# Attention maxima: one head in a slot of one bank, four slots, in place of two heads in a slot of two banks, two slots

## The reference

```python
x = x + _L0_attn_ref(_layernorm(x), Wq_down, Wk_down, Wv_down, Wq_up_c, ..., Wv_up, Wc)
x = x + _L0_ffn_ref(_layernorm(x), Wr, br, W1, b1, W2, b2)

# in the attention, for each batch and head (q, k, v from latent projections, half of q and k with rope)
scores = einsum('bhqd,bhkd->bhqk', q, k) / sqrt(16)
scores = where(causal, scores, -inf)
att = softmax(scores, axis=-1)
y = einsum('bhqk,bhkd->bhqd', att, v)
```

## Time and profile before

| | us |
|---|---|
| three runs | 2732.42, 2733.09, 2741.71 |
| their median | 2733.09 |
| profiled execution, span from the first to the last instruction | 2735.5 |
| attention in it, about | 258 to 1941 |

### The profile page before, as it was taken

The page is one execution under the profiler, slowest core; times in us unless marked ns, Lnnn a source line. Parts: engine busy times, 40 slices in busy tenths (PEclk is TensorE's granted clock), DMA queues, the critical chain, the costliest instruction groups (busy, mean ns, idle before and its releaser), DMA issues. The chain is left out here.

```text
span 2735.5 us, 48214 instructions
## 1 busy us (share of the span) xinstructions
PE 2406.9 (88%) x15842; PEld 1359.7 (50%) x15842; DVE 2048.1 (75%) x5002; ACT 1581.1 (58%) x2716; POOL 823.7 (30%) x1130
## 2 busy tenths in 40 slices
PE   6885799999999999999999999998777389998998
PEld 6774333333334333333334333332444278887897
DVE  3876989998999898888898998940355457765776
ACT  3663277777777776667777777776433234433443
POOL 1543011211212112111212112121055655555554
PEclk8997699999999999989999999997888689999999
DMA  3777814414504513504414423010675323323332
GB/s 145 261 260 212 113 39 63 74 42 61 86 29 64 86 34 59 84 27 65 83 35 64 80 44 71 8 31 20 236 203 177 94 92 113 107 93 96 111 109 72
DMA packets 147501, 255.95 MB, mean 94 GB/s; under 512 B 72951, under 2 KB 91897, under 8 KB 138916
## 3 DMA queue, kind: packets, MB, share of 16 engines
q1 hardware_dynamic: 114544, 164.96, 27.1%
q0 software_dynamic: 29904, 80.65, 8.9%
q10 hardware_dynamic: 2812, 7.26, 1.5%
HBM read 147.59 MB, written 107.76 MB: 93 GB/s over the span
## 5 line engine op out<-in xcount | busy, mean ns | idle before, releaser
L836 ACT ACTIVATE prob<-ps_s 128x512 f32<-128x512 f32 (+5 forms) x1620 | 1078.1, 714 | 480.5 <-PE ps_s L932 477.8
L857 DVE TENSOR_REDUCE maxes<-ps_m 128x2 f32<-128x1024 f32 x768 | 913.9, 1221 | 107.8 <-PE ps_m L973 104.8
L932 PE MATMUL ps_s<-q_st,k_st 50*128 50x512 f32 (+3 forms) x2560 | 610.2, 413 | 73.8 <-ACT prob L836 57.2
L973 PE MATMUL ps_m<-k_st,q_st 48*128 48x512 f32 (+3 forms) x2560 | 603.2, 443 | 75.9 <-DVE maxes L857 39.6
L953 PE MATMUL ps_o<-prob,v_sb 128*17 128x512 f32 (+3 forms) x5120 | 617.5, 556 | 1.2 <-ACT prob L836 0.7
L802 POOL TENSOR_SCALAR_AFFINE_SELECT prob<-prob 128x256 f32<-128x256 f32 x512 | 203.2, 406 | 1347.8 <-ACT prob L836 1220.8
L973 PEld LDWEIGHTS ps_m<-k_st,q_st 48*128 48x128 f32 x2560 | 272.6, 191 | 531.3 <-DVE maxes L857 256.6
L861 DVE CUSTOM_DVE_ANT_0 junk<-ps_m,causal 128x128 f32<-128x128 f32 (+3 forms) x1024 | 453.1, 484 | 44.2 <-PE ps_m L973 42.7
L932 PEld LDWEIGHTS ps_s<-q_st,k_st 50*128 50x128 f32 x2560 | 318.3, 190 | 306.1 <-ACT prob L836 234.1
L1728 ACT ACTIVATE h_hi<-ps_turned 128x512 fp32r<-128x512 f32 x142 | 85.0, 598 | 225.6 <-PE ps_turned L1843 157.9
L94 PE MATMUL ps_out<-experts_hi,h_lo 128*128 (+1 forms) x568 | 173.0, 305 | 0.0
(11 more groups left out here) (187 smaller groups left out, 3180.6 us busy)
## 6 DMA issues: line engine op xcount, KB each, us to landing
parts_dram<-parts SPq DMA_DIRECT2D x64, 512.0 KB, 3.8
q_st<-parts_dram SPq DMA_DIRECT2D x84, 256.0 KB, 8.5
k_st<-parts_dram SPq DMA_DIRECT2D x84, 256.0 KB, 18.4
v_dram<-v_out SPq DMA_DIRECT2D x16, 544.0 KB, 5.5
xin<-in_L_attn_x SPq DMA_DIRECT2D x16, 512.0 KB, 6.0
ffn_raw<-in_L_ffn_W POOLq DMA_DIRECT2D x32, 256.0 KB, 5.2
y_dram<-y_sb SPq DMA_DIRECT2D x64, 128.0 KB, 2.0
split_hi<-ffn_hi POOLq DMA_DIRECT2D x16, 512.0 KB, 3.2
```

What stands on the lines that cost most here:

```text
L836: last_exp = nc.scalar.activation(prob[:, at:at + n, lo:TB], bank[:, 0:n, lo:TB], ACT.Exp, scale=DH ** -0.5)
L857: return nc.vector.tensor_reduce(maxes[:, 2 * pair:2 * pair + 2, qt, kc], bank[:, :, :], AX.X, ALU.max)
L932: mm = nc.tensor.matmul(ps_s[k % 2][:, i, lo:TB], k_st[half(h % 2, ROWS), w % BUFS, h // 2, kt * P:(kt + 1) * P], q_st[half(h % 2, ROWS), ...
L973: mm = nc.tensor.matmul(ps_m[slot][:, i, 0:wide], q_st[half(i, STACK), w % BUFS, pair, qt * P:(qt + 1) * P], k_st[half(i, STACK), w % BUFS ...
```

## The change

A piece of the maxima is now one head: ("max", w, qt, h, kc), with the two heads of a pair one after the other. TensorE makes one matmul for it into a slot of one bank and signals it. VectorE takes it with one tensor_reduce of 128x512 or one masked reduction, and signals it. The ring has four slots of one bank. turn_max stands four pieces into the next turn. The planner models pieces of one head, in the half of TensorE's rows that belongs to the head. The number and shape of the matmuls, of the masked reductions, of the scores and of the sums are the same; the 768 reductions of 128x1024 become 1536 of 128x512. turn_max and turn_out use one bank of a slot, as they did before.

```diff
--- before.py
+++ after.py
@@ -466,10 +466,10 @@
 HALF_ROWS = 64
 EARLY = 12
 NEG = -3.0e38
-SLOTS = 2
+SLOTS = 4
 PROBS = 6
 DEEP = 3
-AHEAD = 2
+AHEAD = 4
 BUFS = 3
 HOLD = {"max": -171, "scores": -140, "sum": 0, "turn_out": -266}
 STEP_LIST = [(w, c, kt) for w in range(NG) for c in range(CH)
@@ -502,7 +502,8 @@
     out = []
     for i, (w, late) in enumerate(turns):
         tiles = range(EARLY, QT) if late else range(EARLY)
-        pieces = [("max", w, qt, pair, kc) for qt in tiles for pair in range(2) for kc in range(qt // TILES + 1)]
+        pieces = [("max", w, qt, h, kc) for qt in tiles for pair in range(2) for kc in range(qt // TILES + 1)
+                  for h in (2 * pair, 2 * pair + 1)]
         turn = [("turn_max",) + turns[i - 1]] if i else []
         out += pieces[:AHEAD] + turn + pieces[AHEAD:] + [("chain", w, late)]
     return out + [("turn_max",) + turns[-1]]
@@ -575,9 +576,8 @@
                 rows[e[1:]] = vector + 6500
             else:
                 w = piece_width(e[2], e[4])
-                end = max(columns(0, w, ready[kind]), columns(1, w, ready[kind]))
-                vector = max(end + 42, vector - 85) + (2 * w * 1.049 + 148 if e[4] < e[2] // TILES else
-                                                       2 * (w * 1.045 + 152) - 83)
+                end = columns(e[3] % 2, w, ready[kind])
+                vector = max(end + 42, vector - 85) + (w * 1.049 + 148 if e[4] < e[2] // TILES else w * 1.045 + 152)
             taken.append(vector)
         elif kind == "scores":
             plan.append(("scores", k))
@@ -643,7 +643,7 @@
         rec = sb("rec", [P, 2, TILES, GH], F32)
         ident = sb("ident2", [P, P], F32)
         causal = sb("causal", [P, TB], F32)
-        junk = sb("junk", [P, SLOTS, 2, TB], F32)
+        junk = sb("junk", [P, SLOTS, TB], F32)
         maxes = sb("maxes", [P, GH, QT, CH], F32)
         minus = sb("minus", [P, GH * EARLY], F32)
         ones = sb("ones", [PARTS, T], F32)
@@ -653,7 +653,7 @@
         minus_rows = sb("minus_rows", [GH * EARLY, PARTS, P], F32R)
 
         ps_s = [ctx.enter_context(nc.psum_tensor(f"ps_s{i}", [P, 2 - i, 512], F32)) for i in range(2)]
-        ps_m = [ctx.enter_context(nc.psum_tensor(f"ps_m{i}", [P, 2, 512], F32)) for i in range(SLOTS)]
+        ps_m = [ctx.enter_context(nc.psum_tensor(f"ps_m{i}", [P, 512], F32)) for i in range(SLOTS)]
         ps_o = ctx.enter_context(nc.psum_tensor("ps_o", [P, 512], F32))
 
         ident_made = sem("ident_made2")
@@ -851,17 +851,13 @@
 
             def take(e, slot):
 
-                _, _, qt, pair, kc = e
+                _, _, qt, h, kc = e
                 bank = ps_m[slot]
                 if kc < qt // TILES:
-                    return nc.vector.tensor_reduce(maxes[:, 2 * pair:2 * pair + 2, qt, kc], bank[:, :, :], AX.X,
-                                                   ALU.max)
+                    return nc.vector.tensor_reduce(maxes[:, h, qt, kc:kc + 1], bank[:, :], AX.X, ALU.max)
                 w = piece_width(qt, kc)
-                for i in range(2):
-                    last = nc.vector.tensor_tensor_reduce(junk[:, slot, i, 0:w], bank[:, i, 0:w],
-                                                          causal[:, TB - w:TB], 1.0, NEG, ALU.add, ALU.max,
-                                                          maxes[:, 2 * pair + i, qt, kc:kc + 1])
-                return last
+                return nc.vector.tensor_tensor_reduce(junk[:, slot, 0:w], bank[:, 0:w], causal[:, TB - w:TB], 1.0,
+                                                      NEG, ALU.add, ALU.max, maxes[:, h, qt, kc:kc + 1])
 
             for e, ring in plan_with_ring():
                 slot = ring % SLOTS
@@ -883,14 +879,14 @@
                     if j:
 
                         dve.wait_ge(rows_in, 32 * j)
-                    nc.vector.tensor_copy(minus_rows[0:n, 0, :], bank[0:n, 0, 0:P]).then_inc(high_made, 1)
+                    nc.vector.tensor_copy(minus_rows[0:n, 0, :], bank[0:n, 0:P]).then_inc(high_made, 1)
                     dve.wait_ge(high_made, j + 1)
-                    nc.vector.tensor_tensor(out=minus_rows[0:n, 1, :], in0=bank[0:n, 0, 0:P],
+                    nc.vector.tensor_tensor(out=minus_rows[0:n, 1, :], in0=bank[0:n, 0:P],
                                             in1=minus_rows[0:n, 0, :].bitcast(F32),
                                             op=ALU.subtract).then_inc(piece_taken, 1)
                 elif e[0] == "turn_out":
                     c, made = e[1] % 2, e[1] // 2
-                    src = ps_m[slot][:, 0, :].rearrange("p (j h d) -> p j h d", j=TILES, h=GH)
+                    src = ps_m[slot][:, :].rearrange("p (j h d) -> p j h d", j=TILES, h=GH)
                     dve.wait_ge(piece_made, ring + 1)
                     nc.vector.reciprocal(rec[:, c, :, :], src[:, :, :, DH]).then_inc(rec_made, 1)
                     dve.wait_ge(rec_made, e[1] + 1)
@@ -960,7 +956,7 @@
                     if ring >= SLOTS:
                         pe.wait_ge(piece_taken, ring - SLOTS + 1)
                     if e[0] == "max":
-                        _, w, qt, pair, kc = e
+                        _, w, qt, h, kc = e
                         if w == 0 and chunks_seen <= qt // TILES < 2:
                             pe.wait_ge(chunk_loaded[chunks_seen], (LOADS - 1) * 16)
                             chunks_seen += 1
@@ -969,19 +965,18 @@
                             pe.wait_ge(loaded[w % BUFS], LOADS * 16 * (w // BUFS + 1))
                             loads_seen = w + 1
                         wide = piece_width(qt, kc)
-                        for i in range(2):
-                            mm = nc.tensor.matmul(ps_m[slot][:, i, 0:wide],
-                                                  q_st[half(i, STACK), w % BUFS, pair, qt * P:(qt + 1) * P],
-                                                  k_st[half(i, STACK), w % BUFS, pair, kc * TB:kc * TB + wide],
-                                                  start=True, stop=True)
+                        mm = nc.tensor.matmul(ps_m[slot][:, 0:wide],
+                                              q_st[half(h % 2, STACK), w % BUFS, h // 2, qt * P:(qt + 1) * P],
+                                              k_st[half(h % 2, STACK), w % BUFS, h // 2, kc * TB:kc * TB + wide],
+                                              start=True, stop=True)
                     elif e[0] == "turn_max":
                         n = GH * (QT - EARLY if e[2] else EARLY)
                         pe.wait_ge(minus_made, turn_number(e[1], e[2]) + 1)
-                        mm = nc.tensor.transpose(ps_m[slot][0:n, 0, 0:P], minus[:, 0:n], ident[:, :])
+                        mm = nc.tensor.transpose(ps_m[slot][0:n, 0:P], minus[:, 0:n], ident[:, :])
                     else:
                         pe.wait_ge(out_copied, e[1] + 1)
                         for j in range(TILES):
-                            mm = nc.tensor.transpose(ps_m[slot][:, 0, j * P:(j + 1) * P],
+                            mm = nc.tensor.transpose(ps_m[slot][:, j * P:(j + 1) * P],
                                                      out_sb[:, e[1] % CH, j * P:(j + 1) * P], ident[:, :])
                     mm.then_inc(piece_made, 1)
 
```

## The result

Before 2732.76 us (median of 4 runs), after 2843.49 (2821.78 to 2860.64, 4 runs): a ratio of 1.0398, interval 1.0322 to 1.0473. I had said 2707, with a range of 2655 to 2768. The profiled execution has a span of 2858.9 us, 123 more than before.

The account below looks back on a forecast made before the run. The chain of scores, exponentials and sums was taken to bound the kernel. 2735.5 - 28 (slots) + 1.5 (VectorE) = 2709 us, as a median 2707; own range 2690 to 2722, over all cases 2655 to 2768.

Parts of the forecast that it names:

- the part on TensorE: TensorE's matmuls: number and sizes unchanged, parted pairs 0, newly computed planner order 0 with 10 us either way.
- What bounds the kernel: Attention: the chain of scores, exponentials and sums sets the end; maxima matter where they hold up TensorE's queue.
- the 51 us: VectorE: two reductions of 512 add 0.066 us per full pair, 51 us of work, only 1.5 us on the path.
- The slots: PSUM slots for maxima: banks freed one reduction earlier remove three quarters of TensorE's 37.2 us idle time, 28 us.
- Rival 2: TensorE: sums or scores between a pair's heads cost 0.10 us each, 43 us for a third of pairs; chance 0.14.

Follow-up runs that it names:

- -100: Changed kernel with the planner's allowance for maxima (HOLD) at -100 instead of -171, run twice: 0.9847 and 0.9876 of the kernel before.
- the pair order: Changed kernel's single-head slots with the old planner's list, each pair written as its two heads in a row: 0.9945, repeated on another chip 0.9991.
- -150: Changed kernel with the planner's allowance for maxima (HOLD) at -150 instead of -171: 1.0122 of the kernel before.
- the full dose: Single-head slots, old list, even heads of two successive pieces put before the odd ones, 1764 same-half neighbours instead of 682: 1.0308 of the kernel before.
- the postponed sums: Kernel before, from step 40 each sum with step number a multiple of 8 put back until just before the next sum: 1.037.
- -171: The changed kernel as it stands, with the planner's allowance for maxima (HOLD) at -171: 1.0398 of the kernel before.
- two doses: Single-head slots, old list, heads regrouped by half in every couple of pieces (1.0308) or only in every second couple (1.0126).

## Why the prediction was wrong

- *The step that failed* is the last of the part on TensorE: "The planner's order is computed anew with the same holds, and may shift some groups; I count this at 0 with 10 us either way." It was worth more than 110 us. With the old list the same slots cost nothing (0.9945 and 0.9991), with the new one 4.0%. I had treated HOLD as a constant of the kernel. It is a credit for each piece, and the change halved the piece; with -100 in its place the changed kernel is at 0.985 to 0.988.
- *What bounds the kernel* was right: the chain of steps sets the end, and VectorE's reductions don't. The two reductions cost +0.4% at the most likely, and the 51 us were 962.7 - 913.9 = 49.
- *The slots* were over-priced. TensorE's idle time for VectorE fell as forecast, from 37.2 us to 3.4 in the pair order (its rows above and 0.4 before the output transpose), but from 320 to 1815 us the busy time of the maxima matmuls rose by 57 us (566.3 to 622.8) and that of TensorE as a whole by 29, and the time fell by 0.1 to 0.55%, not 1%. That the two heads' banks now come free 0.60 us apart, so that the second matmul starts later behind the first, would explain it; this is argued, not tested.
- *Rival 2* (parted pairs) named a real cost, but as 43 us in the worst case and at 0.10 us each, where 0.065 to 0.09 in all and 0.05 at the full clock were measured. The changed kernel has 432 more same-half neighbours: 22 us at the 0.05, about half of the 47 us in slower steps. Even that half is not shown. At -150, with 1077 neighbours, a step takes 2.48 us at the full clock, as before the change, and at -100, with 978, only 2.41.
- *The clock* stood in no rival, though the two windows of before (0.98 in the middle part, 0.79 in the tail) showed that it is not constant in this kernel. Two thirds of the loss or more stand there.
- *Open*: how much of the clock's part is due to long stretches and how much to same-half neighbours (the full dose and the postponed sums had one without the other, and both had more falls), and what makes -171 so much worse than -150, where the profiled execution has 14 falls and 122 us at the lower level in its middle part. That the order of the list costs the time is shown; which feature of it costs how much is not.

The page "TensorE: Matmul & The Clock Gate" of the Trainium skill describes (section "A second HAM failure mode: psum-queue depth-cycling") a clock that swings because TensorE idles for a moment between groups of matmuls. The trace agrees in part only: before the fall shown above the idle rows are 0.17 and 0.20 us, and the middle part as a whole is busier than before the change (1546.08 of 1585 us). What was missing ahead of most of its falls was sums, not busy time; that this is the cause was not isolated.

## What to carry to other kernels

When a list is written by a planner, changing the size of a piece changes the planner: re-set the allowances before judging the change, and count in the new list what went with the loss here: stretches without full-array work, neighbours in one half of the array, and a lead at the buffers' limit. To price the hardware side alone, run the new mechanism with the old order first. That one run told more than all of the arithmetic on slots.

## What the runs showed of the hardware that I had not expected

TensorE's clock fell to 1.2 GHz 35 times in a stretch in which it was shown busy for 97.5% of the time, and 11 times where it was busy for 93%. Two neighbouring matmuls in one half of the rows, instead of in different halves, cost 0.05 us more at the full clock, at two doses, and 0.065 to 0.09 with what the clock took. A reduction out of PSUM that waits for its own semaphore still overlaps the one before it by 0.08 us (0.68 us each, a start every 0.60).
